# Two-stage MoE routing: idle-operand matmuls in TensorE's gaps, slots ahead of weights, first expert product ahead of the second turn

## What is computed

```python
x = x + attention(layernorm(x))            # 16 heads, cumulative state
xf = layernorm(x)
scores = softmax(xf @ w_cls.T)             # 32 routed + 32 zero experts
_, topk_idx = top_k(scores + bias, 8)
w = take(scores, topk_idx); w = w / (w.sum(-1) + 1e-20) * 1.5
# every routed expert e < 32 takes its tokens in order, at most 256:
buf[e, pos] = xf[token]
g, u = split(buf[e] @ w_gate_up[e]);  y = (silu(g) * u) @ w_down[e]
x = x + (sum of w * y over a token's routed experts) * (1 + sum of its zero-expert weights)
```

## Time and profile before

| what | value |
|---|---|
| median of 3 runs | 1025.31 us (1025.07, 1025.31, 1026.66) |
| span of the profiled execution, first to last instruction | 1019.6 us |
| that execution's own time | not listed apart from the three; the median is 5.7 us over the span |
| mean granted TensorE clock | 0.957 |
| PE busy | 909.3 us (89%) |
| DVE busy | 766.4 us (75%) |
| ACT busy | 503.8 us (49%) |
| POOL busy | 494.5 us (48%) |
| moved by DMA | 131.03 MB |

### The profile page before, as it was taken

The page is one execution under the profiler, slowest core; times in us unless marked ns, Lnnn a source line. Parts: engine busy times, 40 slices in busy tenths (PEclk is TensorE's granted clock), DMA queues, the critical chain, the costliest instruction groups (busy, mean ns, idle before and its releaser), DMA issues. The chain is left out here.

```text
span 1019.6 us, 14540 instructions
## 1 busy us (share of the span) xinstructions
PE 909.3 (89%) x4377; PEld 736.6 (72%) x4377; DVE 766.4 (75%) x1821; ACT 503.8 (49%) x867; POOL 494.5 (48%) x420
## 2 busy tenths in 40 slices
PE   4789999999999999999799999999759988697960
PEld 3577888888888888888578888888547666475850
DVE  6977988888888888888877777776577967586730
ACT  5454555555555555554652222222237867575730
POOL 2466766666667666666500000000046456667652
PEclk9999999999999999999999999999859999798995
DMA  8001111111111111112653653431149999898743
GB/s 296 6 32 47 58 37 58 47 58 42 51 54 46 48 48 58 42 48 86 262 193 133 257 194 127 142 136 65 64 149 286 330 287 269 227 276 262 216 64 41
DMA packets 52759, 131.03 MB, mean 129 GB/s; under 512 B 12156, under 2 KB 14588, under 8 KB 46528
## 3 DMA queue, kind: packets, MB, share of 16 engines
q1 hardware_dynamic: 41248, 114.67, 32.1%
q0 software_dynamic: 11424, 15.29, 8.3%
HBM read 106.53 MB, written 35.91 MB: 140 GB/s over the span
## 5 line engine op out<-in xcount | busy, mean ns | idle before, releaser
L595 POOL TENSOR_TENSOR a_t<-a_t 128x512 f32<-128x512 f32 x80 | 105.1, 1314 | 101.8 <-DVE a_t L358 101.8
L1076 DVE TENSOR_TENSOR w_l<-raw,w_h 128x1024 fp32r<-128x1024 f32 x96 | 114.8, 1222 | 13.4 <-ACT w_h L1069 11.7
L604 POOL TENSOR_TENSOR a_fQ<-a_fQ,a_den 128x512 f32<-128x512 f32 x64 | 88.0, 1376 | 71.8 <-DVE a_den L396 71.8
L213 PE MATMUL a_PQ<-w_h,a_xT_h 128*128 128x512 f32 x384 | 106.7, 400 | 10.3 <-DVE w_l L345 9.6
L775 PE MATMUL r_PY<-w_h,r_o_h 128*128 128x512 f32 x256 | 106.5, 416 | 3.4 <-DVE r_o_l L866 3.4
L1046 POOL TENSOR_SCALAR r_vr<-r_mv 128x1 f32<-128x1 f32 x16 | 8.4, 525 | 205.3 <-DVE r_mv L877 205.3
L1174 POOL DMA_INDIRECT out<-m_y,si x38 | 66.0, 1736 | 78.9 <-DMA out<-m_y,si 51.7
L213 PE MATMUL a_PQ<-w_l,a_xT_h 128*128 128x512 f32 x384 | 103.7, 392 | 0.0
L213 PE MATMUL a_PQ<-w_h,a_xT_l 128*128 128x512 f32 x384 | 103.5, 392 | 0.0
L775 PE MATMUL r_PY<-w_h,r_o_l 128*128 128x512 f32 x256 | 101.9, 398 | 0.0
L1069 ACT ACTIVATE w_h<-raw 128x1024 fp32r<-128x1024 f32 x96 | 97.8, 1054 | 8.1 <-DMA m_ident<-in_cr 7.8
(11 more groups left out here) (169 smaller groups left out, 2184.7 us busy)
## 6 DMA issues: line engine op xcount, KB each, us to landing
raw<-in_wgu SPq DMA_DIRECT2D x32, 1024.0 KB
oT<-a_o SPq DMA_DIRECT2D x64, 256.0 KB, 2.4
raw<-in_wd SPq DMA_DIRECT2D x32, 512.0 KB
v_l<-oT SPq DMA_DIRECT2D x11, 1024.0 KB, 7.1
v_h<-oT SPq DMA_DIRECT2D x5, 1024.0 KB, 6.5
out<-r_x SPq DMA_DIRECT2D x18, 256.0 KB, 2.0
a_xin<-in_x SPq DMA_DIRECT2D x16, 256.0 KB, 3.0
v_l<-in_wq SPq DMA_DIRECT2D x4, 1024.0 KB, 12.6
```

Source lines behind the costliest of these rows:

```text
L213: last = eng.matmul(bank[:, :], a[:, k, :], w[:, 4 * i + k, :], start=s == 0 and k == 0, stop=s == 2 and k == 3)
L595: eng.tensor_tensor(t1[:, r % 2, :], t1[:, r % 2, :], t2[:, r % 2, :], ALU.add).then_inc(sm["xr"], 1)
L604: eng.tensor_tensor(q, q, den[:, n % 2, :].unsqueeze(2).broadcast_to([P, 4, P]), ALU.mult).then_inc(sm["fs"], 1)
L1076: eng.tensor_tensor(low, src, high.bitcast(F32), ALU.subtract).then_inc(sm["m_wl"], 1)
```

## The change

Three edits:

1. A helper `keep_warm(n)` puts `n` matmuls of 128 rows by 512 columns on two finished tiles (`o_h`, fp32r) into TensorE's list, with their result in a PSUM bank of its own, `PW`, that nobody reads. They wait for nothing. They stand only in the routing block's closing part: 6 after `table(14)`, 5 after `turn(15)`, 8 after `logits(15)`, 10 after `ranks(15)`, 8 after `table(15)`, and 22 behind the last four matmuls, as the last work of TensorE in the block; 59 in all.
2. On VectorE, in chunk 15 alone, `slots(c)` stands ahead of `weights(c)`.
3. In the experts' loop, in iteration 0 alone, TensorE's `up(0)` (both tiles) stands ahead of `turn(1)`.

```diff
-        PX, PR, PK, PB = ps("PX"), ps("PR"), ps("PK"), ps("PB")
+        PX, PR, PK, PB, PW = ps("PX"), ps("PR"), ps("PK"), ps("PB"), ps("PW")
...
+                def keep_warm(n):
+
+                    for _ in range(n):
+                        eng.matmul(PW[:, :], o_h[:, 0, 0:P], o_h[:, 1, 0:512], start=True, stop=True)
+
...
                 table(NC - 2)
+                keep_warm(6)
                 turn(NC - 1)
+                keep_warm(5)
                 logits(NC - 1)
+                keep_warm(8)
                 ranks(NC - 1)
+                keep_warm(10)
                 table(NC - 1)
+                keep_warm(8)
                 eng.wait_ge(sm["r_L"], 1)
                 for g in range(4):
                     last = eng.matmul(PX[:, 16 * g:16 * g + 16], L[:, g, :, :].rearrange("p a b -> p (a b)"), sel_r[:, :],
                                       start=g == 0, stop=g == 3, skip_group_check=True)
                 last.then_inc(sm["r_tt"], 1)
+                keep_warm(22)
...
                     choose(c)
-                    weights(c)
-                    slots(c)
+                    if c < NC - 1:
+                        weights(c)
+                        slots(c)
+                    else:
+                        slots(c)
+                        weights(c)
...
                     both(eng, regs, e - 1, turn_a, "m_at1")
+                    if e == 0:
+                        both(eng, regs, 0, up, "m_gu1")
                     both(eng, regs, e + 1, turn, "m_xt1")
-                    both(eng, regs, e, up, "m_gu1")
+                    if e > 0:
+                        both(eng, regs, e, up, "m_gu1")
                     both(eng, regs, e - 1, down, "m_yd1")
```

## The result

The changed kernel takes 1030.3 us in the median against 1024.7 us for the kernel before, timed on the same chip in 12 runs each. One run of the changed kernel took 3192.3 us and is left out of the ratio. The ratio is 1.0060, 95% interval 1.0035 to 1.0086: 6.1 us slower, between 3.6 and 8.8 (the two medians lie 5.6 us apart). The forecast was 1030.7 us.

The account below looks back on a forecast made before the run. Bound: the experts' chain of scatters, paced by landings and started by expert 0's output, with routing's closing part ahead. Barrier +3.4 and experts +2.0 gave +5.4 on 1025.3: 1030.7 us; 8-in-10 range 1022.0 to 1036.0.

Parts of the forecast that it names:

- The gaps: Routing's closing part: matmuls in PE's idle gaps hold the clock without delay; turn -0.49, logits' end -1.83 us.
- Part 2: Routing, chunk 15: slots ahead of weights brings table(15) earlier on PE, but VectorE has the same work, so nothing gained.
- part 1: Routing's closing part: 59 idle-operand matmuls keep the clock up, logits' end -1.83 us, but the closing 22 delay the barrier.
- The 22 hold the barrier: Routing's end: closing DRAIN waits for the 22 matmuls; +2.1 us if the clock holds, +4.7 if not, +3.4 taken.
- the upper price: Routing's closing barrier: about +4.7 us if the clock falls ahead of the last four matmuls.
- The queue: Routing's closing barrier: the DRAIN waits for queued work, although 22 matmuls' 44 entries would fit a depth of 64.
- The first rival: Routing's end: barrier opens with the 22 still running, early product pays; -4.7 us, 1020.6 us, chance 0.20.
- Part 3: Experts' first iteration: product 2.4 us earlier but silu pushed back; first scatter +3.7 to +5.4 us, +2.0 taken in total.
- the fill isn't waited for: Routing's end: barrier opens when VectorE is done, 2.3 us earlier; -4.7 us in all, 1020.6 us, chance 0.20.
- they cancel: Barrier and experts' start: a loss at one offsets a gain at the other; 1025.0 us, chance 0.13.
- the early fall of the clock: Routing's closing part: clock falls anyway, each matmul group outlasts its gap; about +14 us, 1039 us, chance 0.05.

Follow-up runs that it names:

- part 1 alone: All 59 idle-operand matmuls added to the kernel before, nothing else changed: ratio 1.0012 (0.9981 to 1.0043).
- 44: The changed kernel with 44 closing matmuls in place of 22: timed once, 1034.95 us.
- Part 3 alone: The kernel before with only expert 0's first product moved ahead of the second turn on TensorE: ratio 1.0029 (1.0007 to 1.0050).
- the 37 and part 2: The kernel before plus the idle-operand matmuls in the gaps, without the closing 22, and slots ahead of weights in chunk 15: ratio 0.9995 (0.9968 to 1.0023).

## Why the prediction was right

The forecast, 1030.7 us and slower, came true (1030.3), and in the main for its own reasons. That the two agree to 0.4 us is luck: the measured loss is known to 2.6 us on either side, and two of the terms were choices inside wide ranges. Step by step:

- **The gaps.** Forecast -0.49 at the turn and -1.83 at the logits' end, no group of the 37 in the way. Measured 0.46 for the turn, the logits 1.53 in place of the 1.42 taken from chunk 14, and the first step on the table 13.95 us behind the last projection against 743.10 - 727.36 = 15.74: -1.8, as summed. Only table(15) follows the group ahead of it without a gap, and VectorE needed its result later.
- **Part 2 nothing.** Shown by itself. Beside part 1 it costs 0.3 at the end of the table, and with it PE's gap ahead of the last four is 2.29 us in place of 0.78. The prediction saw this gap (2.2 us) and priced the clock's fall behind it, but did not put it down to part 2.
- **The 22 hold the barrier.** Forecast +2.1 if the clock holds and +4.7 if it falls, +3.4 taken. In the changed kernel the clock fell in both executions, for some 3.4 us, and the term was +3.7 each time. It held only in part 1 alone (+1.8), which has the smaller gap. The middle value was taken because the fall was open; it came close since the upper price was 1.0 too high. Of this, 0.5 is that the last four matmuls still ran at full clock (0.61), and 0.4 that the fall cost the 22 only 1.6 us (6.85 against 5.26) in place of 2.
- **The queue.** The DRAIN rows of 22 and of 44 end with the last matmul, and the barrier opens behind them. The Trainium skill, "TensorE: Matmul & The Clock Gate", opening table, gives TensorE's queue a depth of 64. The first rival drew from this depth that the barrier could open with the 22 still running; the page itself doesn't say so, and at this block's end the depth was no cover.
- **Part 3.** Product 2.6 us earlier (forecast 2.4), silu 3.5 us later (3.2 to 4.8), PE idle for 4.47 us (4.5), clock down at up(1). First scatter +3.4 with the change and +3.8 alone, against +3.7 to +5.4. What stays open is the share that reaches the end: +2.0 was taken from a range of nothing to 5.4. Part 3 alone lost 3.0 us (0.7 to 5.1) in the total. The pair of kernels with the 37 and part 2, with and without part 3, shows none. The 2.0 lies between and is neither confirmed nor refuted.

The stages gave +7.1 up to the first scatter where the sum had +5.4 for the whole, and the total shows 6.1. Over all timed kernels the totals go the way of the stage sums with somewhat less than their size: +7.1 gave +6.1, +6.7 gave +5.9, +3.6 gave +3.0, +2.9 gave +1.2, +0.6 gave -1.2, -0.2 gave -1.5, -2.0 gave -0.9, -2.6 gave -0.5, -3.0 gave -0.5 and -4.8 gave -4.7. Each total has an interval of some 2 to 3.5 us on either side, and whether the experts' stage absorbs a part or none of a shift is not settled by these runs. Nor is it shown that its scatters run at the pace of landings alone: in the profile before, POOL was idle 51.7 us ahead of scatters for a landing, and another 23.8 us, in 15 waits, for which the profile names no releaser.

The rivals: "the fill isn't waited for" is refuted by the DRAINs, "they cancel" by both, the ratios and the first scatter; the early fall of the clock occurred in no profiled execution with the 37.

## What to carry to other kernels

Work put into an idle engine is free only as long as something else that everybody waits for ends later anyway. Behind the last useful instruction of a block that cover was 0.8 us here, and the closing DRAIN waited for all 5 to 7 us of it, and everybody for the DRAIN. And a step that is moved forward on one engine pays only if the lists of the engines that consume it are moved as well: in-order lists turned a product that was 2.6 us early into a silu that was 3.5 us late; moved on three engines it was a gain of 2.0 us up to the first scatter. The idle-operand matmuls in the gaps bring the barrier 2.2 us forward here, a gain that the total of that kernel by itself doesn't tell from nothing; and no clock was carried over the 5 us for which PE stands idle behind the barrier.

## What the runs showed that I had not expected

PE's sequencer was ahead of its array by the same amount in two kernels. Its DRAIN begins at 743.9 with 22 matmuls (part 1 alone), 1.0 us behind the first of them, and at 751.4 with 44, 7.3 us behind; in both it then lasts 4.24 us. At 0.234 us a matmul that is an estimated 18 matmuls with their 18 weight loads still ahead of the DRAIN, and these rows read as a sequencer that is held up until no more than these are left.

Two edits that look independent met in the clock. Slots first is worth nothing on VectorE and makes PE's table earlier, and just that opened a gap of 2.29 us on PE ahead of the last four routing matmuls, against 0.78 us in part 1 alone. The fall at 742 in the changed kernel (in the window above) and the slower 22 (6.85 against 5.26 us) came with the wide gap. Whether the narrow gap would hold the clock in every execution isn't known from the one that was profiled.
